# In the last step of each image, products 4 and 5 and products 7 and 8 are added by accumulating transfers, in a fused two-layer convolution kernel

## The reference

```
value = (x @ vp_w + vp_b).reshape(n, h, w, G, GC)
...
sampled = ((1 - ty) * (1 - tx))[..., None] * v00 + ... + (ty * tx)[..., None] * v11
out = jnp.einsum('nhwgkc,nhwgk->nhwgc', sampled, mask).reshape(n, h, w, c)
return out @ op_w
```

## Time and profile before

| what | us |
|---|---|
| median of 3 runs (3767.25 to 3767.76) | 3767.26 |
| the profiled execution's own time | 3762.78 |
| its span in the trace | 3761.0 |
| an image's last step, images 0 to 6 | 102.7 to 103.1 |
| the next image's first step | 100.5 to 101.1 |
| an image's third step (j = 2) | 97.8 |

### The profile page before, as it was taken

How to read it: one execution, slowest core, us unless ns; L and a number is a source line. 1 busy time by engine, 2 the same in 40 slices (tenths; PEclk the granted TensorE clock), 3 DMA queues, 4 the chain that set the end, 5 groups by cost and what they waited for, 6 DMA issues and landing times. The chain is left out here.

```text
span 3761.0 us, 89283 instructions
## 1 busy us (share of the span) xinstructions
PE 3499.6 (93%) x36672; PEld 2250.2 (60%) x36672; DVE 3365.7 (89%) x2555; ACT 2549.4 (68%) x4937; POOL 622.6 (17%) x476
## 2 busy tenths in 40 slices
PE   4899999999999999999999999999999999858998
PEld 2566666666666666666666666666666666623333
DVE  4799899999999899989998999999998999948776
ACT  5677677777776677667776777777766666345554
POOL 0011111101111111111111111011111111104444
PEclk9999999999999999999999999999999999979999
DMA  6566676666666666667666766666666665436553
GB/s 176 123 139 123 136 158 151 131 134 145 146 139 134 126 149 142 131 132 153 149 128 136 157 143 134 139 138 146 141 130 120 129 129 101 86 151 225 210 209 147
DMA packets 329155, 537.40 MB, mean 143 GB/s; under 512 B 38268, under 2 KB 243708, under 8 KB 314760
## 3 DMA queue, kind: packets, MB, share of 16 engines
q0 software_dynamic: 103296, 263.22, 38.1%
q1 hardware_dynamic: 224584, 266.07, 24.1%
q10 hardware_dynamic: 832, 2.10, 0.2%
HBM read 262.53 MB, written 67.41 MB: 88 GB/s over the span
## 5 line engine op out<-in xcount | busy, mean ns | idle before, releaser
L1104 DVE TENSOR_TENSOR pv<-val,wsum 128x2048 f32<-128x2048 f32 x800 | 1809.0, 2284 | 139.0 <-PE ps_add L864 122.2
L864 PEld LDWEIGHTS ps_add<-ident,pv 128*128 128x128 f32 x11776 | 1282.4, 141 | 293.7 <-issue 205.3
L864 PE MATMUL ps_add<-ident,pv 128*128 128x128 f32 x11776 | 1390.8, 275 | 36.2 <-DVE pv L1104 33.9
L816 PE MATMUL ps_om<-xdw,omw 128*32 128x256 f32 x13824 | 868.0, 384 | 97.9 <-ACT hat L615 96.7
L816 PEld LDWEIGHTS ps_om<-xdw,omw 128*32 128x32 f32 x13824 | 391.2, 109 | 418.6 <-ACT hat L615 146.8
L613 ACT ACTIVATE hat<-ps_om,omb 128x256 f32<-128x256 f32 x576 | 275.1, 478 | 394.7 <-PE ps_om L816 375.1
L1043 DVE TENSOR_TENSOR prod<-hat,mwy 128x1536 f32<-128x1536 f32 (+1 forms) x272 | 347.7, 1312 | 43.8 <-DMA wsum<-prod 33.1
L787 PE MATMUL ps_bg<-tri,diag 128*32 128x512 f32 x3024 | 345.8, 591 | 12.1 <-ACT tri L579 12.1
L568 ACT ACTIVATE tri<-tri,gn_tri 96x1024 f32<-96x1024 f32 (+1 forms) x376 | 329.8, 949 | 4.7 <-ACT gn_tri L536 4.4
L1029 DVE TENSOR_TENSOR mwy<-hat,msk 128x768 f32<-128x768 f32 x288 | 273.6, 950 | 55.3 <-ACT hat L627 55.3
L489 POOL DMA_DIRECT2D wsum<-acc x80 | 98.8, 1235 | 1248.7 <-DVE wsum L1043 1248.7
(11 more groups left out here) (153 smaller groups left out, 3256.0 us busy)
## 6 DMA issues: line engine op xcount, KB each, us to landing
tri<-in_x_dram SPq DMA_DIRECT2D x725, 128.0 KB, 3.3
pv<-pv POOLq DMA_DIRECT2D x64, 1024.0 KB, 7.6
wsum<-acc POOLq DMA_DIRECT2D x80, 768.0 KB, 7.3
wsum<-prod POOLq DMA_DIRECT2D x80, 768.0 KB, 7.5
win<-in_x_dram SPq DMA_DIRECT2D x144, 256.0 KB, 3.5
x<-xres SPq DMA_DIRECT2D x128, 256.0 KB, 2.9
xres<-in_x_dram POOLq DMA_DIRECT2D x124, 256.0 KB, 11.0
out_dram<-c_x SPq DMA_DIRECT2D x31, 1024.0 KB, 4.3
```

What stands on the lines that cost most here:

```text
L816: mm = nc.tensor.matmul(ps_om[G * q:G * q + G, (par + i) % 2, 0:TOK], omw[:, h, comp, :], xdw[:, j % 2, h, q, :], start=h == 0, stop=h == ...
L864: mm = nc.tensor.matmul(ps_add[:, tb, c, :], pv[:, (j + uv) % PBUF, c, P * tb:P * tb + P], consts["ident"][:, :], start=uv == ADDED[0] and ...
L1104: nc.vector.tensor_tensor(pv[:, (j + uv) % PBUF, :, :].rearrange("p c (r w) -> p c r w", w=W), val[:, :, SR * j + u:SR * j + u + SR, v:v + ...
```

## The change

In an image's last step (`heavy(j)`), the pairs are 0 into 1, 2 into 3, 4 into 5 and 7 into 8, where the first two were the only ones. PE no longer adds 4 and 7 there. The waits of PE and DVE follow, and the counts behind them are worked out by new helpers. The tables of the other steps, and the order of DVE's instructions, are as before.

```diff
+HEAVY_PAIRED = {5: 4, 8: 7}
 ADDS_AT = [(13, 14, 15), (16, 17, 18), (19, 20, 21), (22, 23, 24), (), (1,), (4, 3, 5, 6), (7, 8, 9), (10, 11, 12)]
...
+HEAVY_ADDS_AT = ADDS_AT[:6] + [(3, 5, 6), (8, 9)] + ADDS_AT[8:]
...
+def heavy(j):
+
+    return j % STEPS == STEPS - 1
+
+
+def paired(j):
+
+    return {**PAIRED, **HEAVY_PAIRED} if heavy(j) else PAIRED
+
+
+def adds_at(j, k):
+
+    return (HEAVY_ADDS_AT if heavy(j) else ADDS_AT)[k]
...
@@ add_pair on POOL @@
                     pool.wait_ge(pv_full, SHIFTS * s + uv + 1)
-                    at_least(pool, pair_added, 16 * (len(PAIRS) * s + PAIRS.index(uv)))
-                    nc.gpsimd.dma_start(pv[:, (j + uv) % PBUF, :, :], pv[:, (j + PAIRED[uv]) % PBUF, :, :],
+                    at_least(pool, pair_added, 16 * pairs_before(n, j, uv))
+                    nc.gpsimd.dma_start(pv[:, (j + uv) % PBUF, :, :], pv[:, (j + paired(j)[uv]) % PBUF, :, :],
                                         accum_op=ALU.add).then_inc(pair_added, 16)
...
                                 add_pair(n, j, 3)
+                            if k == 7 and heavy(j):
+                                add_pair(n, j, 5)
                             add_products(n, j, k)
+                        if heavy(j):
+                            add_pair(n, j, 8)
...
@@ add on PE @@
-                    if uv in PAIRED:
-                        pe.wait_ge(pair_added, 16 * (len(PAIRS) * s + PAIRS.index(uv) + 1))
+                    if uv in paired(j):
+                        pe.wait_ge(pair_added, 16 * (pairs_before(n, j, uv) + 1))
...
@@ multiply on DVE @@
+                    used, of = (uv - PBUF, (n, j)) if uv >= PBUF else (uv - PBUF + SHIFTS, previous(n, j))
+                    into = {v: k for k, v in paired(of[1]).items()}
+                    if used in into:
+                        dve.wait_ge(pair_added, 16 * (pairs_before(*of, into[used]) + 1))
+                    elif uv >= PBUF or not is_step(n, j, 0, 0):
+                        dve.wait_ge(add_done, adds_before(*of) + added(of[1]).index(used) + 1)
```

More of the change, by code:

```diff
@@ L40 @@
 PAIRED = {1: 0, 3: 2}
-PAIRS = list(PAIRED)
+HEAVY_PAIRED = {5: 4, 8: 7}
 ADDS_AT = [(13, 14, 15), (16, 17, 18), (19, 20, 21), (22, 23, 24), (), (1,), (4, 3, 5, 6), (7, 8, 9), (10, 11, 12)]
-ADDED = [uv for k in (4, 5, 6, 7, 8, 0, 1, 2, 3) for uv in ADDS_AT[k]]
-ADDS = len(ADDED)
+HEAVY_ADDS_AT = ADDS_AT[:6] + [(3, 5, 6), (8, 9)] + ADDS_AT[8:]
 SENT_TAPS = (1, 2, 3, 6, 7)
@@ L70, in following, with added, pairs_before, adds_before @@
     return (n, j + 1) if j < STEPS - 1 else (n + 1, 0)
+def heavy(j):
[4 more added lines that the diff above has]
+    return (HEAVY_ADDS_AT if heavy(j) else ADDS_AT)[k]
+def added(j):
+    return [uv for k in (4, 5, 6, 7, 8, 0, 1, 2, 3) for uv in adds_at(j, k)]
+def pairs_before(n, j, uv):
+    return n * sum(len(paired(i)) for i in range(STEPS)) + sum(len(paired(i)) for i in range(j)) + sorted(paired(j)).index(uv)
+def adds_before(n, j):
+    return n * sum(len(added(i)) for i in range(STEPS)) + sum(len(added(i)) for i in range(j))
 def previous(n, j):
@@ L628, in hats, with summed @@
                                          scale=-1.0).then_inc(hat_full, 1)
-                def summed(s):
-                    act.wait_ge(add_done, ADDS * (s + 1))
+                def summed(n, j):
+                    act.wait_ge(add_done, adds_before(*following(n, j)))
                     for tb in range(TB):
@@ L726, in step @@
                             act.wait_ge(wsum_added, 16 * (sent_before(TAPS) * s + sent_before(4)))
-                            summed(s - 1)
+                            summed(*previous(n, j))
                         if k + 2 < TAPS:
@@ L765, in _ @@
                 statistics(NI - 1, STEPS - 2, (0, 1))
-                summed(STEPS * NI - 1)
+                summed(NI - 1, STEPS - 1)
                 at = unit(NI - 1, STEPS - 1, "project3", NI) + 1
@@ L852, in group_mean, with add @@
                                      start=True, stop=True).then_inc(bg_full, 2)
-                def add(s, j, uv):
-                    if uv in PAIRED:
-                        pe.wait_ge(pair_added, 16 * (len(PAIRS) * s + PAIRS.index(uv) + 1))
+                def add(n, j, uv):
+                    s, order = STEPS * n + j, added(j)
+                    if uv in paired(j):
+                        pe.wait_ge(pair_added, 16 * (pairs_before(n, j, uv) + 1))
                     else:
                         pe.wait_ge(pv_full, SHIFTS * s + uv + 1)
-                    if uv == ADDED[0]:
+                    if uv == order[0]:
                         at_least(pe, add_out, s)
@@ L864, in add @@
                             mm = nc.tensor.matmul(ps_add[:, tb, c, :], pv[:, (j + uv) % PBUF, c, P * tb:P * tb + P],
-                                                  consts["ident"][:, :], start=uv == ADDED[0] and c % 4 == 0,
-                                                  stop=uv == ADDED[-1], is_transpose=True, skip_group_check=True)
+                                                  consts["ident"][:, :], start=uv == order[0] and c % 4 == 0,
+                                                  stop=uv == order[-1], is_transpose=True, skip_group_check=True)
                     mm.then_inc(add_done, 1)
@@ L886, in add_next @@
                     def add_next(k, early):
-                        before = [uv for uv in ADDS_AT[k][:1] if uv not in PAIRED]
-                        for uv in before if early else ADDS_AT[k][len(before):]:
+                        before = [uv for uv in adds_at(j, k)[:1] if uv not in paired(j)]
+                        for uv in before if early else adds_at(j, k)[len(before):]:
                             if k >= SAMPLED:
-                                add(s, j, uv)
+                                add(n, j, uv)
                             elif not first:
-                                add(s - 1, j - 1, uv)
+                                add(*previous(n, j), uv)
                     def place(name):
@@ L932, in _ @@
                 for k in range(SAMPLED):
-                    for uv in ADDS_AT[k]:
-                        add(STEPS * NI - 1, STEPS - 1, uv)
+                    for uv in adds_at(STEPS - 1, k):
+                        add(NI - 1, STEPS - 1, uv)
                 at = unit(NI - 1, STEPS - 1, "project3", NI) + 1
```

## The result

| | us |
|---|---|
| before, median of 5 runs (3765.7 to 3769.5) | 3767.26 |
| changed, median of 5 runs (3781.6 to 3787.4) | 3784.57 |
| ratio, 95% interval | 1.0042 [1.003, 1.0055] |
| span of the profiled executions, before and changed | 3761.0 and 3781.1 |

The prediction was 3766.5 us with a range of 3757 to 3778, and it was wrong: the kernel is 17 us slower. The profiled executions differ by 20.1 us, and the trace shows where. First the same stretches as in the earlier trace rows, of the changed kernel: the last step of image 1 and the first of image 2, then the last of image 2 and the first of image 3 (columns as there: us, then busy time by engine, granted clock, DMA share, GB/s).

What follows compares the result with a forecast made beforehand. PE was taken to bound last steps and the first steps after them. Removed adds (2.75 us) were nearly given back in waits for pairs: seven times -0.1 makes -0.7 us, against the runs' median 3766.5 us, range 3757 to 3778.

Steps and rivals of the forecast that it cites:

- What bounds the kernel: PE bounds an image's last step and the next first step, DVE the others; PE's arrival at tap 8 counts.
- what the removed adds are worth: Two PE adds removed in each last step, worth 2.75 us if PE waits for nothing new.
- the walk: PE followed instruction by instruction through taps 6 and 7 of a last step; tap 8 reached at 1262.16, before 1262.27.
- DVE's forecast lead of 1.1 us: DVE gets product 7's buffer for product 11 1.1 us earlier; given back in the next step's 6.3 us of waits.
- landing with 7.2 us: Pair of 7 and 8, tap 7: lands at 1258.52, 7.2 us after issue; PE stands 1.46 us.
- the residual no longer mixes in: Tap 7: the four residual issues now stand behind the second pair; used as an argument against that pair landing late.
- The slower rival: The second pair queues behind tap 7's product transfers; at 9.3 us to landing 2.0 us lost per step, 3781 us; chance 0.20.
- -0.1: Each of seven last steps: PE reaches tap 8 0.1 us earlier than before.
- some tenths: Last image's last step: PE is not the bound, and DVE's own short wait changes by some tenths of a us.
- The rule weighed: Skill's estimate of 2.0 us plus bytes over 436 GB/s, 4.4 us per pair; PE would not wait; not used in the sum.

Runs made afterwards that it cites:

- 16 fillers: The changed kernel with 16 more PE transposes of the identity before the add of 8, in place of standing; 3781.43 us, 1.0038 to the kernel before.

## Why the prediction was wrong

**What bounds the kernel and what the removed adds are worth: right.** With nothing in their place the two adds bring PE to tap 8 2.74 us earlier, against 2.75 in the walk, and both steps are 2.7 us shorter. The issue of the second pair came where the walk had it. That PE's arrival at tap 8 counts and DVE's end of the step does not, the two versions with the add of 8 in tap 8 show: their last steps are longer than before (103.5 and 103.7 us in the mean, against 103.0) and the first steps behind them shorter (98.1 and 98.2 against 100.7). In the changed kernel PE's delay reaches DVE by another way than forecast: in the first step of image 3 its waits for PE's adds are 5.7 us (6.3 before), and its waits for ACT, which has its offsets from PE, rise from 0.7 to 3.4. DVE's forecast lead of 1.1 us did not come about: it made product 11 at 1265.26, less 5.35 is 1259.91, against the old 1259.6.

**The step that failed is the landing of the second pair**, "landing with 7.2 us". It measured 8.4 to 9.2 us, 8.6 in the mean. By the walk this is 1.4 us a step, about 10 us. Two things are in it. The prediction dismissed the residual's four transfers, which the change itself moved behind the pair ("the residual no longer mixes in"). Over all the runs, 56 second pairs with them behind took 8.4 to 10.1 us, 8.5 in the median, and 14 with them held back 6.9 to 9.2, 7.9 in the median. So they account for about 0.6 us. The rest is the choice of 7.2, "near the least", where even the held pairs took 7.9 in the median; why these scatter stays open. The slower rival had the right place, and it named the four transfers behind the pair too, but its price of 9.3 us came from a transfer with another ahead of it. That its 3781 us lies close to the result is partly luck: at the 8.6 us measured its rule gives 3776, and the rest is the next term.

**A term was missing: the granted clock.** I read 1.00 in the earlier trace rows and did not ask what a PE that now stands between its adds would be granted. It was 0.50 for 3.4 us in six of the seven steps. That costs 1.67 us in five of them. In image 5 it costs some 0.4 us, since PE would have stood for the second pair until about 2475.2 anyway and came at 2475.60. Together that is 9 us. In the step shown, -0.1 + 1.4 + 1.7 gives the 2.97 us of the trace. The Trainium skill, TensorE: Matmul & The Clock Gate, section "HAM oscillation — how this bites in real kernels", describes such a case, a kernel whose clock falls at every wait for a transfer so that the work behind it starts slow. The trace here agrees in that the slow work stands behind such waits. It differs in that not every wait brings a dip, and in the size of the waits: the page draws them at about 3 to 5 us, and here most were 2.1 to 2.4 us. So the page gives a reason to put the term on the list, not its price.

**The last image was not "some tenths".** From its last step to the end the changed kernel takes 597.5 us against 592.6. With no values to make, PE asks for the pairs and DVE makes the products earlier in the step, and the first pair is issued while a weight product is under way: 9.4 us for it and 9.1 for the second. PE stands far longer than in the other images (first two rows), and the clock is down for 10.2 and 6.8 us around these waits. DVE itself waits for 4.0 us in 3183.6 to 3300 us (last two rows) where before it waited for 0.6; that is most of the 4.9 us.

```profile
3261.60 6.23 PE L898 MATMUL ps_add<-ident,pv 128*128 128x128 f32 x32 [7.35 <-DMA pv<-pv]
3273.37 17.77 PE L898 MATMUL ps_add<-ident,pv 128*128 128x128 f32 x144 [5.54 <-DMA pv<-pv]
```

```profile
DVE pv L1139 <- DMA pv<-pv: 2.6, 2, 2.0
DVE pv L1139 <- PE ps_add L898: 1.4, 1, 1.4
```

**The rule weighed.** The 4.4 us, an estimate from the page DMA: Bandwidth & Descriptors of the Trainium skill, section "Anatomy of one DMA — SWDGE (gpsimd) path", are contradicted here. Of the 80 pairs of the changed kernel none landed under 7.0 us after issue, the median is 7.7, and the slowest took 10.6.

**The sum.** The last step and the first after it take 2.7 us more in seven images, 19 us. The end is 4.9 us longer, and the eight second steps happened to be 4.6 us shorter in all. Together that is 19.4 us, against 20.1 in the spans.

**What stays open:** why the second steps of images 0 to 6 take 98.6 us in the mean in most profiled executions and up to 99.7 in others (99.1 in that of the kernel before). In the longer ones DVE waits longer for weight products, whose issue stands at the same place in the step. The kernels with one pair or with 16 fillers had the long ones, the one with the residual held back, on the same chip, the short ones. With one profile of nearly every kernel this can't be told apart from an effect of the edit, though no edit touches these steps. Between the shortest and the longest lie 9 us in all, as much as several of the differences above. The three forecasts that came out 5 to 6 us too high may owe it to this.

## What to carry to other kernels

On the engine that bounds the kernel, work handed to a transfer is gained only if the engine asks for the result after it has landed. Put the independent work ahead of the one that waits: the same transfers made the kernel 17 us slower in one order of PE's adds and 18 us faster in another. Read what the change puts behind a transfer in its queue, not only what stands ahead, and price a landing with the median of its kind, not with the least. And where an engine comes to stand, look whether the work behind the wait keeps its speed.

## What was not expected of the hardware

An accumulating transfer of 1 MB within SBUF took 8.4 to 10.1 us (median 8.5, 56 transfers in eight executions) when four more of 256 KB were issued on its queue from 0.5 us behind it, and 6.9 to 9.2 us (median 7.9, 14 transfers in two executions) when they were held back.

TensorE's granted clock fell from 1.00 to 0.50 for 3.4 us in 12 of the 14 such steps of the changed kernel. In most of them PE had stood for 1.4 to 1.6 us and some 13 us later for 2.1 to 2.4 us, in the first images' for 0.9 and 3.4 us, in one for 2.4 us only once. The length of the waits does not decide it by itself. The two steps without a dip had 1.45 and 2.2 us, with the residual held back a step with 1.43 and 2.90 us had none, and with PE's own adds first single waits of 1.94, 1.97 and 2.11 us brought one and waits of 2.07 and 2.67 us did not. Single waits of 0.9 to 1.5 us brought none in seven steps, single waits of 3.8 to 3.9 us one in each of seven. What else decides is open.
